# A selective-scan block on one core: who copies the last column of h to the state

## What is computed

```python
h = _layernorm(x) * (1 + ca) + sa
xp, z = jnp.split(h @ W_in, 2, axis=-1)
u = silu(causal_conv(xp, conv_w, conv_b))
dt_r, Bm, Cm = jnp.split(u @ W_xp, [DT_RANK, DT_RANK + D_STATE], axis=-1)
delta = softplus(dt_r @ W_dt + dt_bias)
dA = exp(delta * A)                    # for each channel e and state n
dBu = delta * Bm * u
# for each step t:  h = dA_t * h + dBu_t ;  y_t = sum over n of h * C_t
y = (y + u * D_skip) * silu(z)
x = x + ga * (y @ W_out)
h = _layernorm(x) * (1 + cb) + sb
gate = sigmoid((h @ Wq.T) @ routers.T)           # 255 nodes of a tree of depth 8
x = x + gb * ((leaf_probs(gate) @ leaf_values) @ Wout_w.T + Wout_b)
```

## Time and profile before

| | |
|---|---|
| median of 3 runs | 555.55 us (553.75 to 557.4) |
| the profiled execution | 554.37 us, of it 552.5 us from the first to the last instruction |
| granted TensorE clock, mean | 0.904 of 2.4 GHz |
| VectorE busy | 469.5 us, 85% |
| GpSimd busy | 449.7 us, 81% |
| ScalarE busy | 379.4 us, 69% |
| TensorE busy | 418.0 us, 76% |

### The profile page before, as it was taken

How to read it: one execution, slowest core, us unless ns; L and a number is a source line. 1 busy time by engine, 2 the same in 40 slices (tenths; PEclk the granted TensorE clock), 3 DMA queues, 4 the chain that set the end, 5 groups by cost and what they waited for, 6 DMA issues and landing times. The chain is left out here.

```text
span 552.5 us, 6977 instructions
## 1 busy us (share of the span) xinstructions
PE 418.0 (76%) x2238; PEld 295.5 (53%) x2238; DVE 469.5 (85%) x561; ACT 379.4 (69%) x685; POOL 449.7 (81%) x323
## 2 busy tenths in 40 slices
PE   8978846986697679965897679865996676567776
PEld 5436534754464466744674466634674465446453
DVE  5788789999999789988998789989998799999203
ACT  2367785589758875779668975879667964854460
POOL 3558699977996999879996999789986999799800
PEclk9989977997999889987998889987998897769989
DMA  6491062206220443005230342005230533000001
GB/s 171 122 337 45 6 209 95 77 2 214 95 77 1 135 175 95 2 6 209 97 95 1 145 166 95 1 13 201 97 95 1 190 120 95 2 0 20 0 1 38
DMA packets 22372, 48.98 MB, mean 89 GB/s; under 512 B 4281, under 2 KB 13504, under 8 KB 18240
## 3 DMA queue, kind: packets, MB, share of 16 engines
q1 hardware_dynamic: 22336, 48.54, 25.8%
HBM read 45.91 MB, written 2.62 MB: 88 GB/s over the span
## 5 line engine op out<-in xcount | busy, mean ns | idle before, releaser
L530 POOL TENSOR_TENSOR hc<-h,c_rows 128x1024 f32<-128x1024 f32 x128 | 300.2, 2364 | 46.2 <-DVE h L1181 42.0
L1181 DVE TENSOR_TENSOR_SCAN h<-dA,state,dbu 128x512 f32<-128x512 f32 x192 | 234.6, 1264 | 15.9 <-ACT dA L633 15.4
L633 ACT ACTIVATE dA<-delta,a_neg 128x512 f32<-128x512 f32 x256 | 173.7, 684 | 51.3 <-DVE h L1181 50.8
L1033 PE MATMUL yb<-ident,hc 128*128 128x128 f32 x1024 | 161.2, 298 | 19.3 <-POOL hc L530 19.3
L1033 PEld LDWEIGHTS yb<-ident,hc 128*128 128x128 f32 x1024 | 137.5, 156 | 70.5 <-issue 34.4
L1194 DVE TENSOR_TENSOR dbu<-du,bb 128x1024 f32<-128x1024 f32 x96 | 114.9, 1197 | 13.6 <-PE bb L1010 13.4
L1181 DVE TENSOR_TENSOR_SCAN h<-dA,dbu 128x512 f32<-128x512 f32 x64 | 74.4, 1205 | 10.2 <-ACT dA L633 10.1
L517 POOL TENSOR_TENSOR dbu<-du,b_rows 128x1024 f32<-128x1024 f32 x32 | 75.7, 2364 | 4.6 <-DMA b_rows<-bc_dram 4.1
L1010 PE MATMUL bb<-b_parts,sel 128*128 128x512 bf16 x96 | 41.4, 431 | 24.8 <-DVE dbu L1194 24.0
L921 PE MATMUL mf<-f_hT,w_conv 128*128 128x512 f32 x112 | 56.1, 629 | 2.0 <-ACT zu L691 1.4
L944 PE MATMUL mf<-zu,w_xdt 128*128 128x512 f32 x56 | 37.3, 754 | 25.9 <-ACT delta L738 21.4
(11 more groups left out here) (166 smaller groups left out, 599.6 us busy)
## 6 DMA issues: line engine op xcount, KB each, us to landing
c_rows<-bc_dram SPq DMA_DIRECT2D x32, 1024.0 KB, 6.9
b_rows<-bc_dram SPq DMA_DIRECT2D x32, 256.0 KB, 7.1
xs<-in_L_attn_x_dram SPq DMA_DIRECT2D x8, 256.0 KB, 4.1
out_dram<-xs SPq DMA_DIRECT2D x8, 256.0 KB, 5.4
ygT<-in_L_attn_conv_w_dram SPq DMA_DIRECT2D x1, 512.0 KB, 5.2
bc_dram<-xd SPq DMA_DIRECT2D x8, 64.0 KB, 1.6
probT<-in_L_wmod_dram SPq DMA_DIRECT2D x1, 384.0 KB, 4.1
w_in<-in_L_attn_W_in_dram SPq DMA_DIRECT2D x1, 256.0 KB, 4.3
```

What stands on the lines that cost most here:

```text
L530: nc.gpsimd.tensor_tensor(hc[:, pair % RC, :, :], h[:, pair % RH, :, :], c_rows[:, q, n % NQ, :].unsqueeze(1).broadcast_to([P, HALVES, T]) ...
L633: nc.scalar.activation(dA[ke % RD][:, :], delta[:, ge % 2, half, :], ACT.Exp, scale=a_neg[:, half, n:n + 1]).then_inc(s_dA, 1)
L1033: last = nc.tensor.matmul(bank[:, tile], hc[:, ks // HALVES % RC, half, tile], ident[:, :], start=False, stop=n == N - 1, is_transpose=Tru ...
L1181: v.tensor_tensor_scan(h[:, pair % RH, half, :], dA[k % RD][:, :], dbu[:, pair % RW, half, :], start, ALU.mult, ALU.add).then_inc(s_scan, 1)
```

## The change

GpSimd instead of ScalarE copies the last column of `h` to `state`. The copy stands directly in front of the product of the same pair and shares its wait for the scan. ScalarE's instruction and its wait go. VectorE no longer waits for the copy before it reuses a buffer of `h`: GpSimd's product, for which it still waits, stands behind the copy in GpSimd's own queue. The wait of the next group's scan for the copy stays.

```diff
--- before.py
+++ after.py
@@ -524,6 +524,8 @@
                             pool.wait_ge(s_cld[q], 16 * (g + 1))
 
                         pool.wait_ge(s_scan, HALVES * (pair + 1))
+                        if saved(pair):
+                            nc.gpsimd.tensor_copy(state[:, n, :], h[:, pair % RH, :, T - 1]).then_inc(s_save, 1)
                         if pair >= RC:
 
                             pool.wait_ge(s_sum, HALVES * (pair - RC + 1))
@@ -632,12 +634,6 @@
                             act.wait_ge(s_wdt, 1)
                         nc.scalar.activation(dA[ke % RD][:, :], delta[:, ge % 2, half, :], ACT.Exp,
                                              scale=a_neg[:, half, n:n + 1]).then_inc(s_dA, 1)
-                    if 0 < k < K and k % HALVES == 0 and saved(k // HALVES - 1):
-                        pair = k // HALVES - 1
-
-                        act.wait_ge(s_scan, k)
-                        nc.scalar.activation(state[:, pair % N, :], h[:, pair % RH, :, T - 1],
-                                             ACT.Copy).then_inc(s_save, 1)
                     if g == -1 and s == TR_OF_1:
                         wait_job(act, "f", "z", 1, 0)
                         nc.scalar.activation(f_hT[:, 0:HALO], f_hT[:, T:T + HALO], ACT.Copy).then_inc(s_halo, 1)
@@ -1172,8 +1168,6 @@
                             if pair >= RH:
 
                                 dve.wait_ge(s_hc, pair - RH + 1)
-                                if saved(pair - RH):
-                                    dve.wait_ge(s_save, saves(pair - RH) + 1)
                             if g % CHUNKS:
 
                                 dve.wait_ge(s_save, saves(pair - N) + 1)
```

## The result

Against 20 runs of each, the kernel after took 556.15 us (553.68 to 559.98) and the one before 553.74 us (548.27 to 557.40): ratio 1.0071, 95% interval 1.0041 to 1.0101, so +2 to +6 us (the medians alone are 2.4 us apart). Measured again beside its variants it was 1.0038 (1.0002 to 1.0074). It is slower, by about half a per cent; the forecast was -1.5 us. Executions of one and the same kernel lie up to 9 us apart here at different granted clocks, and a ratio leaves out those more than 1.5% above the fastest of their kernel. The profiled execution, 553.75 us with a span of 552.0, is one of the fastest of its twenty; its span alone would tell of no loss.

A forecast was written before the change was run, and what follows sets the result against it. VectorE was taken as the bound, held up by ScalarE (TensorE behind it) at a few steps per group. ScalarE's -1.8 us plus 0.3 lost in group 6 gave -1.5: 554.0 us, range 550 to 560.

The forecast's parts named there:

- The price of a copy on GpSimd: GpSimd's queue: 0.15 us a copy taken, bounds 0.10 and 0.29; the recorded duration of a tiny instruction was 202 ns.
- No wait at the gates of groups 2, 4 and 5: VectorE's gate after each group: slack of 2.4 to 2.5 us was to cover a 1.9 us push.
- the removed waits and SyncE at nothing: ScalarE's and VectorE's dropped waits were already met, and nothing on SyncE moves: zero cost or gain.
- the short wait forecast: VectorE's gate at the end of group 6: 1.5 + 0.2 against 1.4 us of slack, 0.3 us lost.
- No blocking between GpSimd and VectorE: Rival: a copy stands aside for a running scan, up to 1.26 us, +47 us in all, 603; chance 0.02.
- ScalarE's gain: Copies on ScalarE's unbroken stretches before VectorE's stalls, 0.10 us each: 1.8 us gained; rival of no gain, chance 0.20.
- The push itself: GpSimd from pair 6 to the gate: ten copies, 1.5 us, with VectorE arriving 0.4 us earlier in group 5.
- 1.9 is less than the 2.4 of slack, so the gate doesn't wait; the same in 2 and 4: End of group 5: VectorE's own work up to the gate hides GpSimd's ten copies, at no loss.
- The 0.26 us with which TensorE already waited: TensorE's wait at 400.20 for group 5's last GpSimd product; its sums are awaited by VectorE's gate.
- I set them at no cost: Groups 0 and 1: no leaf products on GpSimd, so it is behind for only part of their last pairs.
- Queued behind a copy are only its own product and what follows on GpSimd: GpSimd's queue: only `dbu` for states 2, 6, 10, 14 and `du` follow; VectorE never waited for either.
- the idle point: GpSimd's 3.72 us of idleness before pair 6's product at 360.05 in group 5; then busy without a gap until 405.67.

The follow-up runs named there:

- The experiment with GpSimd's copies on top: Kernel before, ScalarE's copies kept, plus a GpSimd copy into a spare tile ahead of each saved pair's product: ratio to before 1.0046 (1.0012 to 1.0081).
- the splits of states 0 to 6 and 7 to 15: Kernel before with GpSimd copying only those states, ScalarE the rest: states 0 to 6 0.9965, repeated 0.9969; states 7 to 15 1.0047.
- profiles 3 to 5: Three more profiled executions of the unaltered kernel after: 558.19, 553.05 and 556.26 us.
- the two halves measured apart: Kernel after without any copies or carry between groups, 0.9980; kernel before with extra GpSimd copies into a spare tile, 1.0046; both against before.
- that of states 4 and 6: Kernel before with GpSimd copying only states 4 and 6, ScalarE the fourteen others: ratio to before 1.0060 (1.0023 to 1.0097).
- that of states 0 to 3 and 5: Kernel before with GpSimd copying only states 0 to 3 and 5, ScalarE the others: ratio to before 1.0008 (0.9960 to 1.0055).

## Why the prediction was wrong

Right, by its own steps:

- The price of a copy on GpSimd: 0.15 us taken, 0.14 measured. The bounds and the duration in its place (0.19) would have been worse guides.
- No wait at the gates of groups 2, 4 and 5, and the removed waits and SyncE at nothing. In group 6 even the short wait forecast didn't come; the gate at 464.81 has no bracket. That is in part luck: VectorE lost 0.7 us at step 16 of that group (0.85 to 1.57 us), which gave the last product time.
- No blocking between GpSimd and VectorE: four scans in a row take 4.80 us in both timelines, though the median of their recorded durations rose from 1259 to 1275 ns.
- ScalarE's gain has the expected sign and place (0.63 to 0.47 at step 13, where I had 0.1). Its size is open: about 1 us by the run without copies, for 1.8, with an interval of the difference from -3.2 to +0.9 that holds both 1.8 and nothing.
- The push itself: 1.5 for the copies and 0.4 for VectorE's lead, 1.9 together, measured as 1.8 at the end of group 5 (3.57 to 1.80 us ahead of the gate) and 1.6 at that of group 4 (3.45 to 1.87).

Wrong is the step "1.9 is less than the 2.4 of slack, so the gate doesn't wait; the same in 2 and 4", as the proof that GpSimd's ten copies cost nothing. It followed one consumer of the last product, the sum and VectorE's gate. The 0.26 us with which TensorE already waited was the sign of the other: TensorE had no slack at all there, and its program is in order, so the delay went on into the convolution products, ScalarE's silu and VectorE's step 13. On that path the slack was 0.8 us and not 2.4: the product ended 3.57 us ahead of the gate, and the silu feels it from 2.8 on. 1.8 less 0.8, and less 0.1 that ScalarE's missing copy gives back, is the 0.9 by which the silu is later behind the gate (10.34 to 11.20); the stall grew by 0.7 (0.62 to 1.31 in group 5, 0.63 to 1.32 in group 6), as VectorE itself arrives 0.2 later there. The same step fails in a second place: "I set them at no cost" of groups 0 and 1. Where group 1 ends, the slack was 0.24 us and the push 0.74, and the stall in group 2 grew from 0.63 to about 1.0 in all five profiles. In group 2, on the other hand, ten copies don't pile up at all: GpSimd idles again before the product of pair 14 in the kernel before (0.28 us at 208.46). "Queued behind a copy are only its own product and what follows on GpSimd" names the same gap: I listed what waits behind the copy and not what waits behind the one who waits. The experiment with GpSimd's copies on top puts the loss at 2.5 us instead of 0.3 (and 0.1 without ScalarE's lead), the splits of states 0 to 6 and 7 to 15 put it on the copies behind the idle point.

The sum of the stalls at step 13 over groups 2, 5 and 6 is 1.7 us over before (3.62 against 1.88) in the first two profiles, but only 0.9, 0.4 and 0.4 over in profiles 3 to 5, where other stalls are longer; over all six groups the five profiles are 1.9 to 3.0 us above the one of before. By the two halves measured apart the net would be 1.0026, and the kernel measured 1.0071 and 1.0038, intervals that reach that value or nearly. What lies above it goes with the clock of TensorE in part of the runs. That a late GpSimd makes those low-clock stretches more frequent, through TensorE's longer idling, is argued, not shown, and two splits without a late GpSimd speak against it: that of states 4 and 6 loses 0.6%, and that of states 0 to 3 and 5 has two runs near 560 at a clock of 0.89 (559.95 and 560.44). The cause of this part stays open. So does whether the gain of 0.3% with states 0 to 6 is ScalarE's or owes something to the same effect; two measurements agree on its size.

## What to carry to other kernels

Slack has to be counted along every consumer of what comes later, not only along the one that the profile shows waiting last. An engine that already waits a little for a result, in an in-order program, passes every further delay to whatever it has queued behind that wait. And a small cost on a busy engine is free or not by its place: the same copies lost behind GpSimd's idle point and not ahead of it. A stall is to be read against the engine that stands in it: at step 13 the awaited exponential came no later on the program's clock, and what had changed was how much of VectorE's lead it took away.

A profile is one execution. Here those profiled were several times among the fastest of their kernel, and the loss of half a per cent was seen in the timed runs and in a stretch between two fixed scans, not in the spans. The stall at which it was first explained was long in two profiles of the kernel after and short in two others, so five profiles of one kernel told more than one.

## What the runs showed of the hardware

A GpSimd copy of 128x2 fp32 from two columns 2048 bytes apart is recorded with 193 ns and takes 139 ns of its queue. ScalarE's copy of the same, recorded with 192 ns, took 0.10 us of its queue (373.92 to 374.02 in the earlier trace rows). The granted clock in one and the same stretch of one and the same kernel was 1.00 in one execution and 0.84 in another, 4 us longer, which is more than the change studied is worth.
